# The gap of the matrix rotations: one subtraction on VectorE in place of a matrix product, and a product with A on GpSimd

## Chip, cores and metric

One core of one Trainium2 chip. The metric is the device time in microseconds of one execution of the whole program.

## What is computed

The input is a batch of 16 images with 128 channels of 32x32. Each channel is read as a 32x32 matrix: 2048 matrices. The part that matters here is the first layer of the reference, an eigendecomposition:

```python
def _log_eig(Xf):
    w, V = jnp.linalg.eigh(Xf)
    w = jnp.clip(w, EPS_LOG)
    return jnp.einsum('nij,nj,nkj->nik', V, jnp.log(w), V)
L = _log_eig(Xf)                    # 2048 matrices of 32x32
Lc = gamma * (L - jnp.mean(L, axis=0)) + beta
Y = _exp_eig(Lc)
```

It stands between a group normalisation, and an attention layer (top 32 of 1024 keys) with a mixture of low-rank experts, which the change leaves as they are.

## The kernel before

The stages follow one another, each a block of hand-written engine programs that meet only in semaphores. The stage of the change is `eigen`, from about 245 to 3775 us. It diagonalises all matrices together by **turns**: in each turn, a small rotation is worked out for every matrix from its diagonal and off-diagonal elements, and applied to A (tile `odd`) and to the eigenvectors U (tile `even`). There are 12 turns (`TURNS`) over 32 tiles (`TILES`); a tile has 64 matrices as 128 partitions x 512 columns (four matrices down, 16 across). So there are 384 **slots**, numbered `tau`, and five tiles are in work at once: in slot tau the tile tau has its gaps formed, tile tau-1 its angle (`AT_ANGLE`), tile tau-2 its Gram product (`AT_GRAM`), tile tau-3 its rotation and products (`AT_TURN`), and tile tau-4 is made symmetric again (`AT_SYM`). Turn 11 of the 12 is **mended** (`MEND_AT`, 32 slots): it also restores the orthogonality of U.

Every engine runs its part of the slot in a fixed written order, `slot` on TensorE and `body` on the others, with waits between. The order in a slot without mending:

- TensorE: the product for the rotation's polynomial (`banks[TURN]`, from `zs` and `mix`, L382), the Gram product (x with x, L382), the product of A and the rotation (L382), the gap (L472, L473), the damping (L476, L478), the products that follow (L499). L382 and L499 are 64 products of 32x32 blocks each; the gap and damping products are of full size, 128x128 with 512 columns. The gap bank holds, for each matrix element (i, j), the difference of two diagonal elements: L472 spreads the diagonal over the rows, L473 subtracts it along the columns by a product of minus the identity with `diag_rows`.
- ScalarE: half of the new A (L554), Ln (L557), the new U (L559), Exp (L562), `zs` (L565), the product's copy `prod_u` (L573), the gap's square (L576), the square of the off-diagonal part (L547).
- VectorE: the rotation `j` (L606), `off_rows` (L612), a transpose (L616), `mix` (L619), `rest` (L623), the symmetric A (L627), the angle's tangent `x` = weighed * damped (L634), `weighed` = A * gap (L639), `damped` (L641), `diag_rows` (L593).
- GpSimd: `x_eye` (L663), a copy of U (L668, `u_staged`), a copy of A (L672, `a_staged`), and the masks of the next tile: `diag` (L653) and `off` (L657).

In the mended turn TensorE has two more products, the first of which (`e_flip`) waits for a VectorE transpose (L599) of the copy L668, and the product of A and the rotation comes behind the gap and the damping; L579 copies it out there.

`hold` is a wait that also raises a counter. The loop over the slots is in `through`: the first five slots and the last one of a turn are written out, the others loop.

## Time and profile before

| | |
|---|---|
| median of 3 runs | 9082.76 us (9075.89 to 9084.97) |
| profiled execution | 9074.8 us, its span 9073.1 us |
| TensorE busy | 7923.9 us (87%) |
| VectorE busy | 5380.0 us (59%) |
| ScalarE busy | 3778.8 us (42%) |
| GpSimd busy | 1947.5 us (21%) |
| mean granted TensorE clock | 0.948 |

Busy time is time in which the engine worked on an instruction; the shares are means over stages with different limits. In the rows, PE is TensorE, PEld its load of weights, DVE VectorE, ACT ScalarE, POOL GpSimd. `psum` stands for any bank. A bracket behind a row tells how long the engine had been idle, and what released it.

### The profile page before, as it was taken

How to read it: one execution, taken by the hardware profiler on the slowest of the kernel's cores; microseconds unless marked ns; L12 is line 12 of the kernel's file. 1: busy time of each engine (PE TensorE's matmuls, PEld its weight loads, DVE VectorE, ACT ScalarE, POOL GpSimd, SP SyncE). 2: the span in 40 equal slices, each digit the busy share in tenths (PEclk: the TensorE clock that was granted, in tenths of full speed). 3: DMA queues.
4: the chain of work that ended last, by engine and by line, in shares of the span. 5: the costliest groups of instructions: out<-in, count | busy, mean ns of one | idle time of the engine just before them, and what ended most of it. 6: DMA issues, size and time to landing. Idle time of an engine off the chain costs nothing. (4 is left out here: it accounts for less than half of the span.)

```text
span 9073.1 us, 601301 instructions
## 1 busy us (share of the span) xinstructions
PE 7923.9 (87%) x265196; PEld 4270.7 (47%) x265196; DVE 5380.0 (59%) x15117; ACT 3778.8 (42%) x7262; POOL 1947.5 (21%) x2028
## 2 busy tenths in 40 slices
PE   3999999999999778668856999999999999999998
PEld 2677777777777666557741222222222222222222
DVE  4677777777777546643324555555555555555553
ACT  3455555555555334324422333333334333333333
POOL 1455555555555334300000000000000000000000
PEclk9999999999999889779967999999999999999999
DMA  0000000000000000000010000000000000000000
GB/s 37 1 0 0 0 0 0 0 0 0 0 0 0 0 0 0 1 1 0 0 42 14 15 17 17 12 16 15 13 17 15 17 15 12 17 10 17 15 17 5
DMA packets 58886, 82.10 MB, mean 9 GB/s; under 512 B 26101, under 2 KB 27706, under 8 KB 58426
## 3 DMA queue, kind: packets, MB, share of 16 engines
q1 hardware_dynamic: 58426, 76.45, 3.2%
q8 instruction: 229, 3.75, 0.2%
q14 instruction: 231, 1.89, 0.1%
HBM read 17.63 MB, written 8.39 MB: 3 GB/s over the span
## 5 line engine op out<-in xcount | busy, mean ns | idle before, releaser
L1867 DVE MAX8 w_best<-psum 128x8 f32<-128x128 f32 x8192 | 1725.0, 283 | 1301.9 <-PE psum L1409 1300.5
L1850 ACT ACTIVATE w_exp<-psum 128x512 f32<-128x512 f32 x2048 | 1220.1, 596 | 2291.7 <-PE psum L1418 2289.4
L1428 PE MATMUL psum<-w_exp,w_v 128*32 128x512 f32 x4096 | 2087.6, 608 | 3.0 <-ACT w_inverse L1461 2.7
L1409 PE MATMUL psum<-w_k,w_q 96*128 96x512 bf16 x2048 | 637.3, 394 | 239.7 <-DMA w_k<-w_parts 145.0
L1418 PE MATMUL psum<-w_q,w_k 99*128 99x512 bf16 x2048 | 798.2, 390 | 1.4 <-ACT w_q L1443 1.4
L499 PE MATMUL psum<-e_prod_u,e_j 32*32 32x64 f32 x49152 | 769.8, 215 | 30.5 <-ACT e_prod_u L579 25.1
L499 PEld LDWEIGHTS psum<-e_prod_u,e_j 32*32 32x32 f32 x49152 | 708.0, 105 | 183.2 <-issue 183.2
L1409 PEld LDWEIGHTS psum<-w_k,w_q 96*128 96x128 bf16 x2048 | 123.7, 98 | 1071.4 <-issue 1071.2
L1428 PEld LDWEIGHTS psum<-w_exp,w_v 128*32 128x32 f32 x4096 | 276.0, 108 | 716.8 <-issue 716.8
L653 POOL TENSOR_TENSOR e_diag<-odd,e_eye 128x512 f32<-128x512 f32 x384 | 488.0, 1271 | 559.4 <-PE psum L473 521.3
L547 ACT ACTIVATE e_square<-e_off 128x512 bf16<-128x512 f32 x384 | 242.1, 630 | 844.0 <-POOL e_off L657 844.0
L1418 PEld LDWEIGHTS psum<-w_q,w_k 99*128 99x128 bf16 x2048 | 204.1, 100 | 790.8 <-issue 675.3
L382 PE MATMUL psum<-e_mix,e_zs 32*32 32x32 f32 x49152 | 509.8, 196 | 61.6 <-issue 60.0
L606 DVE TENSOR_TENSOR e_j<-e_rest,psum 128x512 f32<-128x512 f32 x384 | 264.0, 687 | 470.4 <-PE psum L382 470.4
L382 PEld LDWEIGHTS psum<-e_mix,e_zs 32*32 32x32 f32 x49152 | 477.5, 107 | 108.7 <-issue 108.4
L382 PE MATMUL psum<-e_x 32*32 32x32 f32 x49152 | 505.1, 195 | 14.6 <-issue 14.3
L382 PE MATMUL psum<-e_j,e_a_fixed 32*32 32x32 f32 x49152 | 495.9, 194 | 19.6 <-issue 12.7
L951 PE MATMUL psum<-power 32*32 32x32 f32 x28672 | 391.5, 205 | 118.6 <-issue 111.6
L382 PEld LDWEIGHTS psum<-e_j,e_a_fixed 32*32 32x32 f32 x49152 | 462.5, 104 | 62.6 <-issue 28.1
L663 POOL TENSOR_TENSOR e_x_eye<-e_x,e_eye 128x512 f32<-128x512 f32 x384 | 487.8, 1270 | 2.4 <-DVE e_x L634 2.4
L657 POOL TENSOR_TENSOR e_off<-odd,e_not_eye 128x512 f32<-128x512 f32 x384 | 487.9, 1271 | 0.0
L382 PEld LDWEIGHTS psum<-e_x 32*32 32x32 f32 x49152 | 472.5, 106 | 29.6 <-issue 16.3
(268 smaller groups left out, 10889.3 us busy)
## 6 DMA issues: line engine op xcount, KB each, us to landing
w_q<-w_parts SPq DMA_DIRECT2D x768, 32.0 KB, 2.0
w_k<-w_parts SPq DMA_DIRECT2D x768, 32.0 KB, 2.0
odd<-in_x SPq DMA_DIRECT2D x1, 8192.0 KB, 23.1
even<-in_x SPq DMA_DIRECT2D x1, 8192.0 KB, 23.2
out<-w_t SPq DMA_DIRECT2D x16, 512.0 KB, 2.6
w_hid<-in_fc SPq DMA_DIRECT2D x2, 256.0 KB
w_wo<-in_wo SPq DMA_DIRECT2D x8, 8.0 KB
w_wq<-in_wq SPq DMA_DIRECT2D x1, 64.0 KB
```

Of the source, the lines that this page charges most:

```text
L382: last = nc.tensor.matmul(bank[rows, cols], left[rows, cols], right[rows, cols], start=True, stop=True)
L499: last = nc.tensor.matmul(halves(e.pair[:, k // HALF, :])[rows, :, to], e.j[rows, cols], e.prod_u[rows, :, cols], start=True, stop=True)
L606: nc.vector.tensor_tensor(e.j[:], e.rest[:], banks[TURN], ALU.add).then_inc(turned, 1)
L653: nc.gpsimd.tensor_tensor(as_matrices(e.diag[:]), as_matrices(e.a_at(t)), over_matrices(e.eye[:]), ALU.mult)\
L657: nc.gpsimd.tensor_tensor(as_matrices(e.off[:]), as_matrices(e.a_at(t)), over_matrices(e.not_eye[:]), ALU.mult)\
L663: nc.gpsimd.tensor_tensor(as_matrices(e.x_eye[:]), as_matrices(e.x[:]), over_matrices(e.eye[:]), ALU.add)\
L951: last = nc.tensor.matmul(banks[EXP_BANK[n]][rows, S * k:S * k + S], left[rows, k, :], right[rows, k, :], start=True, stop=True)
L1409: last = nc.tensor.matmul(banks[base + k], w.q[0:DEPTH, 4 * g + j, q0:q0 + P], w.k[0:DEPTH, 4 * g + j, half(k)], start=True, stop=True)
L1418: nc.tensor.matmul(banks[4 + x % 2], w.k[0:DEPTH + SHIFT_ROWS, 4 * g + j, P * kt:P * kt + P], w.q[0:DEPTH + SHIFT_ROWS, 4 * g + j, half(qb ...
L1428: nc.tensor.matmul(banks[7][slot(j), :], w.v[:, kt, 4 * g + j, :], w.exp[x % 4][:], start=(kt == 0), stop=(kt == KT - 1)).then_inc(s.weigh ...
L1850: nc.scalar.activation(w.exp[x % 4][:], banks[4 + x % 2], ACT.Exp).then_inc(s.exp_done, 1)
L1867: last = nc.vector.max(w.best[:, i, o, :], banks[o // 4][:, P * (o % 4):P * (o % 4) + P])
```

## The change

The gap no longer ends in an accumulating product. TensorE makes L472's product alone (L477 after); VectorE subtracts `diag_rows` from the bank, spread over the columns, and writes the new tile `gap` (L650). ScalarE squares that tile (L583). GpSimd multiplies A with it (`weighed`, L696), as the last step of its slot, which VectorE did before. On VectorE `x` (L634 in both) moves ahead of `rest` and of the symmetric A, and `diag_rows` (L600 after) ahead of `damped` (L657 after). The tile `minus_ident` and the instruction that fills it are gone, with the counts of the waits around it.

```diff
--- before.py
+++ after.py
@@ -184,7 +184,6 @@
 
     def __init__(self, nc, mem, sb):
         self.block_ones = sb("e_block_ones", [P, P])
-        self.minus_ident = sb("e_minus_ident", [P, P])
         self.damp = [sb(f"e_damp{n}", [P, P], BF16) for n in range(2)]
         self.damp_ident = [sb(f"e_damp_ident{n}", [P, P], BF16) for n in range(2)]
         self.eye = sb("e_eye", [P, S])
@@ -206,6 +205,7 @@
         self.off, self.gap_sq, self.weighed, self.damped = (sb("e_" + n, [P, W]) for n in ("off", "gap_sq", "weighed", "damped"))
         self.half, self.flipped_half, self.flip, self.mend = (sb("e_" + n, [P, W]) for n in ("half", "flipped_half", "flip", "mend"))
         self.prod_u = sb("e_prod_u", [P, 2, W])
+        self.gap = sb("e_gap", [P, W])
         self.square = sb("e_square", [P, W], BF16)
         self.diag_rows = sb("e_diag_rows", [P, TILE])
         self.off_rows = sb("e_off_rows", [P, TILE], BF16)
@@ -265,29 +265,28 @@
             dve.wait_ge(filled, 5)
             folded = "p (q j) -> p j q"
             nc.vector.tensor_reduce(e.eye[:], mem.ident[:].rearrange(folded, j=S), AX.X, ALU.add).then_inc(copied, 1)
-            nc.vector.tensor_scalar(e.minus_ident[:], mem.ident[:], -1.0, None, ALU.mult).then_inc(copied, 1)
             nc.vector.tensor_reduce(e.ramp[:, 0:1], triangle[:], AX.X, ALU.add).then_inc(copied, 1)
-            dve.wait_ge(copied, 3)
+            dve.wait_ge(copied, 2)
...
@@ -453,6 +452,12 @@
         def vectors_at(m):
             return m * 2 + 2
 
+        def mix_at(m):
+            return m * 2 + 1
+
+        def rest_at(m):
+            return m * 2 + 2
+
         def diag_rows_at(m):
             return m * 2 + 1
 
@@ -466,13 +471,13 @@
                 quads(nc, banks[GRAM], e.x, e.x).then_inc(gram_done, 1)
 
             def gaps(m, which, first=False):
-                hold(pe, rows_ready, diag_rows_at(m))
+                hold(pe, diag_ready, m + 1)
+                if not first:
+                    hold(pe, gap_ready, m)
+                nc.tensor.matmul(banks[GAP], e.block_ones[:], e.diag[:], start=True, stop=True).then_inc(gap_done, 1)
+                hold(pe, square_ready, m + 1)
                 if not first:
                     hold(pe, damped, m)
-                nc.tensor.matmul(banks[GAP], e.block_ones[:], e.diag[:], start=True, stop=False)
-                nc.tensor.matmul(banks[GAP], e.minus_ident[:], over_columns(e.diag_rows[:]), start=False, stop=True)\
-                    .then_inc(gap_done, 1)
-                hold(pe, square_ready, m + 1)
                 nc.tensor.matmul(banks[DAMP], e.damp[which][:], e.square[:], start=True, stop=False)
                 hold(pe, rows_ready, off_rows_at(m))
                 nc.tensor.matmul(banks[DAMP], e.damp_ident[which][:], over_columns(e.off_rows[:]), start=False, stop=True)\
@@ -506,7 +511,7 @@
                     if mended:
                         hold(pe, flipped, mended_count(m) + 1)
                         quads(nc, banks[MEND], e.flip, e.flip).then_inc(mend_steps, 1)
-                    hold(pe, mixed, m + 1)
+                    hold(pe, mixed, rest_at(m))
                     quads(nc, banks[TURN], e.zs, e.mix).then_inc(turn_done, 1)
                 if has(AT_GRAM):
                     gram(tau - AT_GRAM)
@@ -572,8 +577,10 @@
                         act.wait_ge(prod_done, m + 1)
                         nc.scalar.activation(e.prod_u[:, 0], banks[PROD], ACT.Copy).then_inc(prod_out, 1)
                 if has(0):
-                    act.wait_ge(gap_done, tau + 1)
-                    nc.scalar.activation(e.gap_sq[:], banks[GAP], ACT.Square).then_inc(gap_squared, 1)
+                    act.wait_ge(gap_ready, tau + 1)
+                    if has(AT_ANGLE):
+                        act.wait_ge(damped, tau - AT_ANGLE + 1)
+                    nc.scalar.activation(e.gap_sq[:], e.gap[:], ACT.Square).then_inc(gap_squared, 1)
                 if has(AT_TURN) and mended:
                     act.wait_ge(prod_done, m + 1)
                     nc.scalar.activation(e.prod_u[:, 0], banks[PROD], ACT.Copy).then_inc(prod_out, 1)
@@ -589,7 +596,7 @@
             def rows(m, first=False):
                 dve.wait_ge(diag_ready, m + 1)
                 if not first:
-                    dve.wait_ge(gap_done, m)
+                    dve.wait_ge(gap_ready, m)
                 nc.vector.tensor_reduce(e.diag_rows[:], as_matrices(e.diag[:]), AX.X, ALU.add).then_inc(rows_ready, 1)
 
             def body(tau, j, has, mended):
@@ -616,8 +623,16 @@
                     nc.vector.transpose(e.flipped_half[:], e.half[:]).then_inc(half_flipped, 1)
                 if has(AT_GRAM):
                     dve.wait_ge(gram_out, tau - AT_GRAM + 1)
-                    nc.vector.scalar_tensor_tensor(e.mix[:], banks[GRAM], FOURTH / THIRD, e.x[:], ALU.mult, ALU.add)
+                    nc.vector.scalar_tensor_tensor(e.mix[:], banks[GRAM], FOURTH / THIRD, e.x[:], ALU.mult, ALU.add)\
+                        .then_inc(mixed, 1)
                     dve.wait_ge(eye_added, tau - AT_GRAM + 1)
+                if has(AT_ANGLE):
+                    dve.wait_ge(inverse, tau - AT_ANGLE + 1)
+                    if has(AT_GRAM):
+                        dve.wait_ge(mixed, mix_at(tau - AT_GRAM))
+                    dve.wait_ge(weighed, tau - AT_ANGLE + 1)
+                    nc.vector.tensor_tensor(e.x[:], e.weighed[:], e.damped[:], ALU.mult).then_inc(angle, 1)
+                if has(AT_GRAM):
                     if has(AT_TURN):
                         dve.wait_ge(turned, tau - AT_TURN + 1)
                     nc.vector.scalar_tensor_tensor(e.rest[:], banks[GRAM], -0.5, e.x_eye[:], ALU.mult, ALU.add)\
@@ -626,21 +641,20 @@
                     dve.wait_ge(half_flipped, tau - AT_SYM + 1)
                     nc.vector.tensor_tensor(e.a_at(tile_of(j, AT_SYM)), e.half[:], e.flipped_half[:], ALU.add)\
                         .then_inc(balanced, 1)
-                if has(AT_ANGLE):
-                    dve.wait_ge(inverse, tau - AT_ANGLE + 1)
-                    if has(AT_GRAM):
-                        dve.wait_ge(mixed, tau - AT_GRAM + 1)
-                    dve.wait_ge(weighed, tau - AT_ANGLE + 1)
-                    nc.vector.tensor_tensor(e.x[:], e.weighed[:], e.damped[:], ALU.mult).then_inc(angle, 1)
+                if has(0):
+                    dve.wait_ge(gap_done, tau + 1)
+                    dve.wait_ge(rows_ready, diag_rows_at(tau))
+                    if has(AT_ANGLE):
+                        dve.wait_ge(gap_squared, tau - AT_ANGLE + 1)
+                        dve.wait_ge(weighed, tau - AT_ANGLE + 1)
+                    nc.vector.tensor_tensor(as_matrices(e.gap[:]), as_matrices(banks[GAP]), over_columns(e.diag_rows[:]),
+                                            ALU.subtract).then_inc(gap_ready, 1)
+                if has(AHEAD):
+                    rows(tau + 1)
                 if has(0):
                     dve.wait_ge(gap_squared, tau + 1)
-                    if has(AT_ANGLE):
-                        dve.wait_ge(angle, tau - AT_ANGLE + 1)
-                    nc.vector.tensor_tensor(e.weighed[:], e.a_at(tile_of(j, 0)), banks[GAP], ALU.mult).then_inc(weighed, 1)
                     dve.wait_ge(damp_done, tau + 1)
                     nc.vector.tensor_tensor(e.damped[:], e.gap_sq[:], banks[DAMP], ALU.add).then_inc(damped, 1)
-                if has(AHEAD):
-                    rows(tau + 1)
 
             rows(0, first=True)
             through(dve, body)
@@ -650,6 +664,7 @@
             def masks(m, t, first=False):
                 if not first:
                     hold(pool, gap_done, m)
+                    hold(pool, rows_ready, diag_rows_at(m - 1))
                 nc.gpsimd.tensor_tensor(as_matrices(e.diag[:]), as_matrices(e.a_at(t)), over_matrices(e.eye[:]), ALU.mult)\
                     .then_inc(diag_ready, 1)
                 if not first:
@@ -660,6 +675,8 @@
             def body(tau, j, has, mended):
                 if has(AT_GRAM):
                     hold(pool, angle, tau - AT_GRAM + 1)
+                    if has(AT_TURN):
+                        hold(pool, mixed, rest_at(tau - AT_TURN))
                     nc.gpsimd.tensor_tensor(as_matrices(e.x_eye[:]), as_matrices(e.x[:]), over_matrices(e.eye[:]), ALU.add)\
                         .then_inc(eye_added, 1)
                 if has(AT_TURN):
@@ -672,6 +689,11 @@
                     nc.gpsimd.tensor_copy(e.a_fixed[:], e.a_at(tile_of(j, AT_GRAM))).then_inc(a_staged, 1)
                 if has(AHEAD):
                     masks(tau + 1, tile_of(j, AHEAD))
+                if has(0):
+                    hold(pool, gap_ready, tau + 1)
+                    if has(AT_ANGLE):
+                        hold(pool, angle, tau - AT_ANGLE + 1)
+                    nc.gpsimd.tensor_tensor(e.weighed[:], e.a_at(tile_of(j, 0)), e.gap[:], ALU.mult).then_inc(weighed, 1)
 
             masks(0, 0, first=True)
             through(pool, body)
```

VectorE, one unmended slot as it is written out, before (the names are written<-read):

```order
L606 TENSOR_TENSOR e_j<-e_rest,psum 128x512
L612 TENSOR_REDUCE e_off_rows<-e_square 128x16
L616 STREAM_TRANSPOSE e_flipped_half<-e_half 128x512
L619 SCALAR_TENSOR_TENSOR e_mix<-psum,e_x 128x512
L623 SCALAR_TENSOR_TENSOR e_rest<-psum,e_x_eye 128x512
L627 TENSOR_TENSOR odd<-e_half,e_flipped_half 128x512
L634 TENSOR_TENSOR e_x<-e_weighed,e_damped 128x512
L639 TENSOR_TENSOR e_weighed<-odd,psum 128x512
L641 TENSOR_TENSOR e_damped<-e_gap_sq,psum 128x512
L593 TENSOR_REDUCE e_diag_rows<-e_diag 128x16
```

and the same slot of the changed kernel:

```order
L613 TENSOR_TENSOR e_j<-e_rest,psum 128x512
L619 TENSOR_REDUCE e_off_rows<-e_square 128x16
L623 STREAM_TRANSPOSE e_flipped_half<-e_half 128x512
L626 SCALAR_TENSOR_TENSOR e_mix<-psum,e_x 128x512
L634 TENSOR_TENSOR e_x<-e_weighed,e_damped 128x512
L638 SCALAR_TENSOR_TENSOR e_rest<-psum,e_x_eye 128x512
L642 TENSOR_TENSOR odd<-e_half,e_flipped_half 128x512
L650 TENSOR_TENSOR e_gap<-psum,e_diag_rows 128x512
L600 TENSOR_REDUCE e_diag_rows<-e_diag 128x16
L657 TENSOR_TENSOR e_damped<-e_gap_sq,psum 128x512
```

There are ten instructions in both; `x` has moved up by two places, the new `gap` stands where `weighed` stood, and `damped` has become the last.

GpSimd, the same slot of the changed kernel (before, the first five of these rows stand there, under L663, L668, L672, L653 and L657):

```order
L680 TENSOR_TENSOR e_x_eye<-e_x,e_eye 128x512
L685 COPY e_prod_u<-even 128x512
L689 COPY e_a_fixed<-odd 128x512
L668 TENSOR_TENSOR e_diag<-odd,e_eye 128x512
L672 TENSOR_TENSOR e_off<-odd,e_not_eye 128x512
L696 TENSOR_TENSOR e_weighed<-odd,e_gap 128x512
```

The sixth row is new, between `off` of this slot and `x_eye` of the next.

## Rows read from the trace of the kernel before

**Rows 1.** Windows: busy time of each engine in two stretches; columns in the first line.
```profile
core 0: us, PE busy (x) PEld busy (x) DVE busy (x) ACT busy (x) POOL busy (x), PEclk, DMA share, GB/s
1330.00:2400.00 1070.00, 1030.07 (x65764) 798.98 (x65753) 796.75 (x1270) 559.87 (x1016) 620.80 (x636) 1.00 0.00 0
2955.00:3470.00 515.00, 379.30 (x24733) 317.22 (x24723) 251.58 (x390) 167.19 (x295) 159.84 (x165) 0.86 0.00 0
```

**Rows 2.** One line's instructions: count, duration ns min/median/max, first and last start.
```profile
L576 ACT ACTIVATE e_gap_sq<-psum x177: 597/597/598, 1425.8 to 2899.0; 128x512 f32<-128x512 f32 x177
...
L579 ACT ACTIVATE e_prod_u<-psum x32: 597/597/598, 2989.4 to 3480.2; 128x512 f32<-128x512 f32 x32
```

**Rows 3.** Timeline, one unmended slot, TensorE: start us, us, engine, line.
```profile
1503.57 1.28 PE L382 MATMUL psum<-e_mix,e_zs 32*32 32x32 f32 x128 [0.16 <-issue]
...
1506.09 1.28 PE L382 MATMUL psum<-e_j,e_a_fixed 32*32 32x32 f32 x128
...
1507.47 1.10 PE L472 MATMUL psum<-e_diag,e_block_ones 128*128 128x512 f32 x2
...
1508.40 1.02 PE L473 MATMUL psum<-e_diag_rows,e_minus_ident 128*128 128x512 f32 x2
...
1509.26 0.38 PE L476 MATMUL psum<-e_square,e_damp 128*128 128x512 bf16 x1
...
1509.79 1.99 PE L499 MATMUL psum<-e_prod_u,e_j 32*32 32x64 f32 x128
...
1511.93 1.28 PE L382 MATMUL psum<-e_mix,e_zs 32*32 32x32 f32 x128 [0.16 <-issue]
```

**Rows 4.** The same timeline, GpSimd.
```profile
1507.63 0.61 POOL L672 COPY e_a_fixed<-odd 128x512 f32 x1 [2.02 <-PE psum L382]
...
1509.69 1.27 POOL L653 TENSOR_TENSOR e_diag<-odd,e_eye 128x512 f32<-128x512 f32 x1 [1.46 <-PE psum L473]
...
1510.92 1.28 POOL L657 TENSOR_TENSOR e_off<-odd,e_not_eye 128x512 f32<-128x512 f32 x1
...
1512.15 1.27 POOL L663 TENSOR_TENSOR e_x_eye<-e_x,e_eye 128x512 f32<-128x512 f32 x1
```

**Rows 5.** The same timeline, VectorE and ScalarE.
```profile
1504.88 0.71 ACT L557 ACTIVATE e_damped<-e_damped,e_floor 128x512 f32<-128x512 f32 x1
1504.89 0.69 DVE L606 TENSOR_TENSOR e_j<-e_rest,psum 128x512 f32<-128x512 f32 x1 [1.18 <-PE psum L382]
...
1507.11 0.69 DVE L619 SCALAR_TENSOR_TENSOR e_mix<-psum,e_x 128x512 f32<-128x512 f32 x1 [0.32 <-ACT e_zs L565]
...
1508.92 0.68 DVE L634 TENSOR_TENSOR e_x<-e_weighed,e_damped 128x512 f32<-128x512 f32 x1
...
1509.46 0.60 ACT L576 ACTIVATE e_gap_sq<-psum 128x512 f32<-128x512 f32 x1 [1.46 <-PE psum L473]
...
1510.20 0.69 DVE L639 TENSOR_TENSOR e_weighed<-odd,psum 128x512 f32<-128x512 f32 x1 [0.60 <-ACT e_gap_sq L576]
```

**Rows 6.** Timeline, three places where GpSimd and VectorE ran at once.
```profile
264.07 1.26 POOL L657 TENSOR_TENSOR e_off<-odd,e_not_eye 128x512 f32<-128x512 f32 x1
264.37 1.52 DVE L634 TENSOR_TENSOR e_x<-e_weighed,e_damped 128x512 f32<-128x512 f32 x1
...
3775.09 0.61 POOL L731 COPY e_a_fixed<-even 128x512 f32<-128x512 f32 x1 [12.32 <-SPq L682]
3775.12 1.12 DVE L701 TENSOR_TENSOR e_zs<-odd,e_eye 128x512 f32<-128x512 f32 x1 [0.33 <-PEq L413]
3775.64 1.07 POOL L731 COPY e_rest<-even 128x512 f32<-128x512 f32 x1
...
3824.55 0.69 DVE L715 TENSOR_TENSOR e_x<-even,e_level 128x512 f32 x1 [3.77 <-PE psum L382]
3824.61 1.11 POOL L731 COPY e_a_fixed<-even 128x512 f32 x1 [47.89 <-PE psum L382]
```

**Rows 7.** Timeline, one slot of the mended turn.
```profile
3223.66 1.29 PE L382 MATMUL psum<-e_j,e_a_fixed 32*32 32x32 f32 x128
...
3229.44 0.61 POOL L668 COPY e_prod_u<-even 128x512 f32 x1
...
3230.94 1.93 PE L382 MATMUL psum<-e_flip 32*32 32x32 f32 x128 [3.22 <-DVE e_flip L599]
```

More of the change, by code:

```diff
@@ L276, in _ @@
             for n, value in enumerate((FIRST_DAMP, LATER_DAMP)):
+                dve.wait_ge(copied, 5 + 3 * n)
+                nc.vector.tensor_scalar(spare[:], mem.ident[:], KAPPA / value, None, ALU.mult).then_inc(copied, 1)
                 dve.wait_ge(copied, 6 + 3 * n)
-                nc.vector.tensor_scalar(spare[:], mem.ident[:], KAPPA / value, None, ALU.mult).then_inc(copied, 1)
+                nc.vector.tensor_tensor(spare[:], spare[:], e.block_ones[:], ALU.add).then_inc(copied, 1)
                 dve.wait_ge(copied, 7 + 3 * n)
-                nc.vector.tensor_tensor(spare[:], spare[:], e.block_ones[:], ALU.add).then_inc(copied, 1)
-                dve.wait_ge(copied, 8 + 3 * n)
                 nc.vector.tensor_scalar(e.damp[n][:], spare[:], value, None, ALU.mult).then_inc(copied, 1)
@@ L284, in _ @@
                 nc.vector.tensor_scalar(e.damp_ident[n][:], mem.ident[:], value, None, ALU.mult).then_inc(copied, 1)
-            dve.wait_ge(copied, 14)
+            dve.wait_ge(copied, 13)
             dve.wait_ge(summed, 1)
@@ L289, in _ @@
                 .then_inc(copied, 1)
-            dve.wait_ge(copied, 15)
+            dve.wait_ge(copied, 14)
             nc.vector.tensor_reduce(e.mirror_rows[:], e.mirror[:].rearrange(folded, j=S), AX.X, ALU.add).then_inc(copied, 1)
@@ L418, in eigen @@
                                                                             "e_rows_ready"))
-        gap_done, damp_done, gap_squared, damped = (sem(n) for n in ("e_gap_done", "e_damp_done", "e_gap_squared",
-                                                                     "e_damped"))
+        gap_done, damp_done, gap_ready, gap_squared, damped = (sem(n) for n in ("e_gap_done", "e_damp_done", "e_gap_ready",
+                                                                                "e_gap_squared", "e_damped"))
         weighed, log_taken, inverse, angle, eye_added = (sem(n) for n in ("e_weighed", "e_log_taken", "e_inverse", "e_angle",
```

## The prediction

> **What bounds the kernel now.** The windows come first, as the page's shares mix stages. In the stretch of unmended turns TensorE is busy for 1030 of 1070 us at a granted clock of 1.00, its upper level, while VectorE has 797 and GpSimd 621 [rows 1]. So look for work that can leave TensorE. In the mended turn TensorE has only 379 of 515 us, at a clock of 0.86: something else sets the pace. The starts of one line give the length of a slot: unmended (2899.0-1425.8)/176 = 8.37 us; mended (3480.2-2989.4)/31 = 15.83 us [rows 2]. Then the timeline of one slot; I count its times from the start of the TURN product, 1503.57. TensorE goes from product to product and has 0.16 us idle in the whole slot, before the next TURN at 8.36 [rows 3]. TensorE bounds 352 of the 384 slots.
>
> **The change, part by part.** *The product L473.* It starts at 4.83 and the damping at 5.69 [rows 3]: its removal frees 0.86 us. The most it can give is the other pair's 0.93 (3.90 to 4.83) [rows 3]. The damping then starts at 4.83, the last product L499 at 5.36 (was 6.22), and the slot is 7.50 long, if nobody else is later. The wait that is added ahead of the damping lies under the gap's product.
>
> *Who else must now fit into 7.50.* GpSimd: the pitch of its big multiplications is 1.23 (1509.69 to 1510.92), a copy takes 0.61 [rows 4]. Before, 3x1.23 + 2x0.61 = 4.9; with `weighed` one more: 6.14. That fits, and `weighed` is a product of the same size; I give it 1.23. A time up to 2.5 would still fit. Queued behind it on GpSimd are `x_eye` and the copies; they have room, as the copy of A waits for the product of A anyway (2.02 us idle before it) [rows 4]. VectorE has ten instructions before and after, at a pitch of 0.61; only `weighed` (0.69, one operand in the bank) turns into the subtraction, same shape, also from the bank, at the same price [rows 5].
>
> *The chain through VectorE and ScalarE.* The gap's end moves from 5.85 (4.83+1.02) to 3.90+1.10 = 5.00 [rows 3]; GpSimd's `diag` started 0.27 behind it [rows 3, 4], so now at 5.27, and ends at 6.54. Chain in the new order: `mix` at 3.54 [rows 5], then `x`, `rest`, A, gap at 0.61 each, the gap's end, square 0.60 and `damped` 0.68 with some 0.1 for the two hand-overs; then from the Ln's start to the next `mix` 2.23 (1504.88 to 1507.11) [rows 5]. Sum 4x0.61 + 0.69 + 0.60 + 0.68 + 0.1 + 2.23 = 6.7, under 7.50. TensorE stays the bound by this count, but it leaves out one thing.
>
> *GpSimd and VectorE at once.* [Rows 6] show that some of their instructions do not overlap. `x`, which has both inputs in SBUF, took 1.52 us instead of 0.68 where it started inside a GpSimd multiplication: that one ended at 265.33, and `x` 0.56 later. The other way round, a GpSimd copy that started 0.06 behind such a VectorE instruction took 1.11 instead of 0.61, until 0.48 after VectorE's end. Before, `x` and the symmetric A run from 1508.32 to 1509.60, in GpSimd's pause (1508.24 to 1509.69) [rows 4, 5]: they never met. Now `x` comes at 4.15, inside the copy of A (4.06 to 4.67), and ends at 5.22. `rest` ends at 5.8; the symmetric A then meets `diag` (5.27 to 6.54) and ends at 7.10. The gap ends at 7.70; `diag_rows` and the square at 8.3; `damped` at 9.1, which is 1.6 of the next slot. There Ln starts at about 1.8 instead of 1.31 (the square of the off part, held back too, and the half of A are ahead of it), `mix` at 4.1, and `x` at 4.7, now free of the copy: the delay does not grow. `j` can start at 1.5 instead of 1.32 and ends at 2.2; the product of A, at 2.52, finds it ready. GpSimd's `off` is held until 7.10, plus 1.14 (1.27 less the 0.13 that the copy in rows 6 saved): 8.24; `weighed`, `x_eye` and the copy of U then end at about 11.2, and the copy of A starts at 7.50+4.06 = 11.56. All fits, with 0.3 us left in the tightest place. The Trainium skill has this as a rule (SBUF — State Buffer, Who interferes with whom): a VectorE instruction with two SBUF inputs contends with a GpSimd instruction that reads SBUF, and the second one blocks fully until the first ends. The trace agrees (1.52 beside 0.68). The rule does not say who goes next when a second GpSimd instruction is queued behind the first.
>
> That is the open point, and one place shows it: a VectorE instruction came at 3775.12 inside a GpSimd copy that ended at 3775.70, the next copy's record starts at 3775.64, and VectorE ended at 3776.24, the second copy at 3776.71 [rows 6]. So VectorE got in between two back-to-back GpSimd instructions. I take that for the forecast. Gain: 352 x 0.86 = 303 us.
>
> *The mended turn.* Its loop runs from the product of A on TensorE through GpSimd (copy of A, `diag`, `off`, `x_eye`, copy of U) and the transpose on VectorE to the first product: 3223.66 to 3230.94, with TensorE idle for 3.22 us at its end [rows 7]. From there TensorE runs through its products to the product of A again. `weighed` now stands in the GpSimd part: +1.23. The pair L473 leaves the TensorE part: -0.86. Per slot +0.37, 32 slots: +12 us. TensorE's pause grows by about a microsecond, and the product after it already runs at the lower level of 1.2 GHz (1.93 us beside 1.28 at the upper) [rows 3, 7]. The bounds of the extra: nothing, or one more product of this kind at the lower level in each slot, 0.65x32 = 21 us. I take the middle, +10, since the pause is only a third longer.
>
> *The rest* (constants, the stages behind) loses one small instruction: nothing. Filling the first slots has a longer latency of a few microseconds, inside the uncertainty.
>
> **Sum.** -303 + 12 + 10 = -281 us. The profiled execution took 9074.8, so 8794; the median is 8 us above it, so 9082.8 - 281 = **8802 us**.
>
> **The rivals.**
>
> *A, slower: GpSimd goes on with what is queued, and the waiting VectorE is let in only when GpSimd stops.* The symmetric A waits until the end of `off`. Counted from the start of `diag`: `off` ends at 2.49, A at 3.04, the gap at 3.64, the square at 4.3, `damped` at 5.0; `j`, queued behind it, runs to 5.69, TensorE takes it 0.15 later, and from the product of A to the next `diag` it is 1.38+1.10+0.27 = 2.75. The loop is 8.59 us, over the 8.37 of now: +0.22x352 = +77, plus 22 for the mended turn, 9182 us. It decides once the symmetric A starts only behind `off`; break-even is at a slot of 8.31. Against it stands the one place at 3775 us; for it, that it is one place, of copies and not multiplications.
>
> *B, a mixed form.* The symmetric A misses its turn in some slots, or another wait eats the 0.3 us. Every second slot in form A gives (7.50+8.59)/2 = 8.05: gain 0.32x352 = 113, less 22: 8992 us. One in three gives 7.86: 8925. For it: little room is left. Against it: a delayed slot gives ScalarE and VectorE a whole microsecond to catch up.
>
> *C, no change.* The product is hidden anyway: that would need TensorE to wait in the slot, and it has 0.16 us of idle time [rows 3]. 9083 us.
>
> *D.* A reader may also fear GpSimd as the new bound. At 6.14 + one blocked instruction's 0.5 it is under 7.50; it would need two more blockings in a slot.
>
> **How the numbers follow.** A measurement of this kernel tells 0.2%, some 18 us, from no change. Forecast (with up to one slot in three late) 0.78; B beyond that 0.08; C 0.03; A, with other mishaps that cost time, 0.11. So faster 0.86, same 0.03, slower 0.11. The low end: 0.93 x 352 = 327 us without any price in the mended turn, 8756, up to 8760. The high end is the mixed form with one in three, 8925, up to 8930. D's chance is inside B.
>
> **What would show it.** Right: a slot of 7.5 us (the starts of the gap's square on ScalarE), TensorE busy in over 95% of the unmended stretch, the damping 0.93 behind the gap's product, the symmetric A with a mean of about 1.3 us instead of 0.68, `weighed` on GpSimd at 1.27, and a mended slot of 16.2 to 16.8. Wrong: idle time before the product of A that `j` ends, or before L657 that the gap's square ends; the symmetric A at over 2 us; a slot of 8.6 us; a GpSimd multiplication with two full inputs of well over 1.27 us. If GpSimd and VectorE do overlap freely, the slot is the same, and only the reasons fail.

## The result and the profile after

The changed kernel takes 8841.12 us (median of 4 runs, 8838.98 to 8844.09), the one before, measured beside it, 9083.59 us. The ratio is 0.9733, with a 95% interval of 0.9721 to 0.9746: 242 us faster. The forecast of 8802 us was 39 us too low; the range (8760 to 8930) holds the result.

The starts of the gap's square on ScalarE, and of the copy of the product of A in the mended turn, in the trace after (they answer to [rows 2]):

```profile
L583 ACT ACTIVATE e_gap_sq<-e_gap x155: 630/631/634, 1421.8 to 2599.3; 128x512 f32<-128x512 f32 x155
...
L586 ACT ACTIVATE e_prod_u<-psum x32: 578/579/597, 2750.2 to 3267.0; 128x512 f32<-128x512 f32 x32
```

An unmended slot is (2599.3-1421.8)/154 = 7.65 us instead of 8.37; a mended one (3267.0-2750.2)/31 = 16.67 instead of 15.83. 352 x 0.72 = 253 us won, 32 x 0.84 = 27 lost: 226, beside 231 by which the spans of the two profiled executions differ (9073.1 and 8842.4). From its first to its last gap's square the stage takes 3479.5 us before (251.3 to 3730.8) and 3247.5 after (249.9 to 3497.4), 232 less; so the 6 us beyond 226 lie inside the stage, outside its regular slots, and the other stages stayed as they were, to within 3 us.

The windows of an unmended stretch and of the mended turn (busy us of each engine, count, then the granted TensorE clock), which answer to [rows 1]:

```profile
1330.00:2200.00 870.00, 816.85 (x58625) 671.55 (x58728) 782.63 (x1139) 482.86 (x912) 750.22 (x684) 1.00 0.00 0
2750.00:3270.00 520.00, 350.32 (x24073) 309.24 (x24096) 241.79 (x374) 156.98 (x281) 191.59 (x190) 0.82 0.00 0
```

GpSimd is busy in 750 of 870 us (86%, was 58%), VectorE in 783 (90%, was 74%), TensorE in 817 (94%, was 96%). Now three engines are nearly full, and each instruction that one of them holds up on another counts.

The timeline of one slot after; its TensorE rows answer to [rows 3], the others to [rows 4, 5]:

```profile
1505.13 0.68 DVE L650 TENSOR_TENSOR e_gap<-psum,e_diag_rows 128x512 f32<-128x512 f32 x1
...
1505.53 1.28 PE L381 MATMUL psum<-e_mix,e_zs 32*32 32x32 f32 x128 [0.18 <-issue]
...
1505.84 0.63 ACT L583 ACTIVATE e_gap_sq<-e_gap 128x512 f32<-128x512 f32 x1 [3.42 <-DVE e_gap L650]
...
1505.91 0.69 DVE L600 TENSOR_REDUCE e_diag_rows<-e_diag 128x16 f32<-128x512 f32 x1
...
1506.51 0.68 DVE L657 TENSOR_TENSOR e_damped<-e_gap_sq,psum 128x512 f32<-128x512 f32 x1
1506.76 1.28 PE L381 MATMUL psum<-e_x 32*32 32x32 f32 x128
...
1507.11 0.68 DVE L613 TENSOR_TENSOR e_j<-e_rest,psum 128x512 f32<-128x512 f32 x1
...
1508.14 1.28 PE L381 MATMUL psum<-e_j,e_a_fixed 32*32 32x32 f32 x128
...
1509.55 1.10 PE L477 MATMUL psum<-e_diag,e_block_ones 128*128 128x512 f32 x2
...
1509.62 0.69 DVE L626 SCALAR_TENSOR_TENSOR e_mix<-psum,e_x 128x512 f32<-128x512 f32 x1 [0.62 <-ACT e_zs L570]
...
1510.52 0.69 DVE L634 TENSOR_TENSOR e_x<-e_weighed,e_damped 128x512 f32<-128x512 f32 x1 [0.20 <-DVE e_mix L626]
...
1510.99 1.34 POOL L668 TENSOR_TENSOR e_diag<-odd,e_eye 128x512 f32<-128x512 f32 x1 [0.79 <-PE psum L477]
...
1511.01 1.99 PE L504 MATMUL psum<-e_prod_u,e_j 32*32 32x64 f32 x128
...
1511.72 1.16 DVE L642 TENSOR_TENSOR odd<-e_half,e_flipped_half 128x512 f32<-128x512 f32 x1
1512.29 1.72 POOL L672 TENSOR_TENSOR e_off<-odd,e_not_eye 128x512 f32<-128x512 f32 x1
1512.81 0.68 DVE L650 TENSOR_TENSOR e_gap<-psum,e_diag_rows 128x512 f32<-128x512 f32 x1
...
1513.17 1.28 PE L381 MATMUL psum<-e_mix,e_zs 32*32 32x32 f32 x128 [0.18 <-issue]
```

From the product of A (1508.14) to L477 it is 1.41 us, from there to L504 1.46, to the next TURN 2.16, and from TURN to the product of A 2.61: 7.64. Before, the same pieces are 1.38, 2.32, 2.14 and 2.52 [rows 3]. So L473's 0.86 is gone in full, and 0.14 has come back, 0.09 of it ahead of the product of A.

### The profile page after: what moved, and what is told of

Read it like the earlier page. It is cut to its first block and busy times, and to the rows that moved or that the text cites. A ratio compares the mean times of both kernels' runs of the same rounds, so it can differ in the third digit from the quotient of the medians.

```text
span 8842.4 us, 603547 instructions
## 1 busy us (share of the span) xinstructions
PE 7580.9 (86%) x264045; PEld 4140.3 (47%) x264428; DVE 5585.1 (63%) x15116; ACT 3724.2 (42%) x7262; POOL 2585.4 (29%) x2412
## 5 line engine op out<-in xcount | busy, mean ns | idle before, releaser
L504 PE MATMUL psum<-e_prod_u,e_j 32*32 32x64 f32 x49152 | 771.3, 216 | 35.7 <-ACT e_prod_u L586 31.6
L504 PEld LDWEIGHTS psum<-e_prod_u,e_j 32*32 32x32 f32 x49152 | 709.2, 105 | 188.9 <-issue 188.9
L583 ACT ACTIVATE e_gap_sq<-e_gap 128x512 f32<-128x512 f32 x384 | 242.3, 631 | 1250.1 <-DVE e_gap L650 1250.1
L672 POOL TENSOR_TENSOR e_off<-odd,e_not_eye 128x512 f32<-128x512 f32 x384 | 643.1, 1675 | 0.0
L668 POOL TENSOR_TENSOR e_diag<-odd,e_eye 128x512 f32<-128x512 f32 x384 | 491.5, 1280 | 310.8 <-PE psum L477 272.5
L680 POOL TENSOR_TENSOR e_x_eye<-e_x,e_eye 128x512 f32<-128x512 f32 x384 | 490.5, 1277 | 0.0
L696 POOL TENSOR_TENSOR e_weighed<-odd,e_gap 128x512 f32<-128x512 f32 x384 | 489.5, 1275 | 3.5 <-DVE e_gap L650 3.5
```

The costliest lines, as they stand in the source:

```text
L504: last = nc.tensor.matmul(halves(e.pair[:, k // HALF, :])[rows, :, to], e.j[rows, cols], e.prod_u[rows, :, cols], start=True, stop=True)
L668: nc.gpsimd.tensor_tensor(as_matrices(e.diag[:]), as_matrices(e.a_at(t)), over_matrices(e.eye[:]), ALU.mult)\
L672: nc.gpsimd.tensor_tensor(as_matrices(e.off[:]), as_matrices(e.a_at(t)), over_matrices(e.not_eye[:]), ALU.mult)\
L680: nc.gpsimd.tensor_tensor(as_matrices(e.x_eye[:]), as_matrices(e.x[:]), over_matrices(e.eye[:]), ALU.add)\
L696: nc.gpsimd.tensor_tensor(e.weighed[:], e.a_at(tile_of(j, 0)), e.gap[:], ALU.mult).then_inc(weighed, 1)
```

## The experiments

A ring is a closed loop of waits that comes back to its own start one slot later; the slot can't be shorter than one round of it. Theory 1: the 0.15 us over the forecast slot are a ring through VectorE (`diag`, symmetric A, gap, `diag_rows`, `damped`, `j`, product of A, gap product, `diag`). Theory 2: they are on TensorE's own queue, the order in which it works off its instructions and waits. Times are medians of the runs, slots from the starts of the gap's square between 1420 and 2600 us, mended slots from the copy of the product of A.

| label | edit | time us | unmended slot | mended slot |
|---|---|---|---|---|
| before | | 9083.6 | 8.37 | 15.83 |
| the change | | 8841.1 | 7.65 | 16.67 |
| x_back | x behind the symmetric A | 8955.9 | 7.98 | 16.61 |
| gap_first | gap ahead of the symmetric A | 8851.3 | 7.69 | 16.63 |
| one_input | symmetric A with one SBUF input | (8859.1) | 7.65 | 16.60 |
| weigh_dve | weighed on VectorE | 9305.1 | 9.08 | 15.46 |
| before_two | before, with the common counter | 9111.0 | 8.48 | 15.46 |
| own_mix | own counter for mix | 8844.8 | 7.68 | 16.35 |
| pool_order | weighed behind the copy of U | 8799.8 | 7.65 | 15.28 |
| own_mix_pool | the last two | 8788.8 | 7.68 | 14.52 |
| own_one | own_mix and one_input | (8806.8) | 7.55 | 16.51 |
| own_a_early | own_mix, symmetric A between mix and x | 8805.2 | 7.55 | 16.46 |
| all_three | own_a_early and pool_order | 8755.4 | 7.55 | 14.94 |

In brackets: the adding of the transpose is left out there, and only one run was timed. The times come from four series on the chip; the kernel before, measured in each, had medians of 9083.6 (the change), 9082.0 (x_back to weigh_dve), 9077.1 (before_two to own_mix_pool) and 9085.6 us (the rest).

**The third part undone: x_back.**

In this diff and those below, a name in capitals stands for the whole block of VectorE's program that forms the tile: `x`, `rest`, the symmetric A (BALANCE), the gap, `diag_rows` (ROWS), `damped`.

```diff
- X; REST; BALANCE; GAP; ROWS; DAMPED
+ REST; BALANCE; X; GAP; ROWS; DAMPED
```

> The angle's x back behind the symmetric A on VectorE; all else as changed. Theory 1: the slot of 7.65 us is a ring through VectorE (diag on GpSimd, symmetric A, gap, diag_rows, damped, j, product of A on TensorE, gap product, diag). Then A starts at 5.3 ahead of diag, but x meets diag and waits until its end near 7.1: the gap ends 0.3 us later, slot 7.9 to 8.0, about 8940 us. Theory 2: TensorE's own queue with its added waits makes the 7.65, the order on VectorE is hidden: slot 7.65, 8841 us.

Measured: slot (2592.7-1420.2)/147 = 7.98 us, 8955.9 us; ratio to before 0.9861 (0.9845 to 0.9878). Theory 1 had the slot (7.9 to 8.0) and the time to within 16 us. The timeline of all three engines:

```profile
1502.19 1.28 PE L381 MATMUL psum<-e_j,e_a_fixed 32*32 32x32 f32 x128 [0.43 <-DVE e_j L613]
...
1504.89 0.68 DVE L636 TENSOR_TENSOR odd<-e_half,e_flipped_half 128x512 f32 x1
...
1505.14 1.56 POOL L668 TENSOR_TENSOR e_diag<-odd,e_eye 128x512 f32<-128x512 f32 x1 [0.79 <-PE psum L477]
...
1505.49 1.76 DVE L643 TENSOR_TENSOR e_x<-e_weighed,e_damped 128x512 f32<-128x512 f32 x1
```

`x` came 0.35 us behind the start of `diag` and took 1.76 us. `diag` itself had come inside the symmetric A and took 1.56. TensorE waits 0.43 us for `j` ahead of the product of A. So moving `x` up is worth 0.33 us in each slot, 115 us of the change's 242: without it the change wins half. That there is a ring through VectorE at 7.98 in this order does not yet say what holds the changed kernel's 7.65.

**The gap ahead of the symmetric A: gap_first.**

```diff
- X; REST; BALANCE; GAP; ROWS; DAMPED
+ X; REST; GAP; BALANCE; ROWS; DAMPED
```

> VectorE's subtraction (gap) ahead of the symmetric A, so that the instruction that GpSimd's diag holds up is no longer ahead of the gap; same instructions. Theory 1 (ring through VectorE): the ring is cut, TensorE's 7.50 us is left: slot 7.50 to 7.55, 352 x 0.12 to 0.15 less, 8788 to 8800 us. Theory 2 (TensorE's own queue): slot 7.65, 8841 us.

Measured: 8851.3 us (8847.4 to 8862.4), slot (2599.7-1423.8)/153 = 7.69. The expectation of theory 1 fell: the ring is shorter, but nothing is won. Of the 150 slots between 1430 and 2590 us, 126 are 7.62 long and 24 are 7.96 to 8.13. Why TensorE gains only 0.02 us in the many is shown further below; what happens in the few is seen in two slots in a row:

```profile
1500.26 0.68 DVE L650 TENSOR_TENSOR odd<-e_half,e_flipped_half 128x512 f32<-128x512 f32 x1
1500.34 1.74 POOL L672 TENSOR_TENSOR e_off<-odd,e_not_eye 128x512 f32<-128x512 f32 x1
...
1508.03 1.27 POOL L672 TENSOR_TENSOR e_off<-odd,e_not_eye 128x512 f32<-128x512 f32 x1
1508.06 1.80 DVE L650 TENSOR_TENSOR odd<-e_half,e_flipped_half 128x512 f32<-128x512 f32 x1
```

In one slot the symmetric A comes 0.08 us ahead of `off` and takes 0.68. In the next it comes 0.03 us behind it and takes 1.80. The 24 slots with the long form (1.79 or 1.80) are the 24 long slots. That is the form of rival B, in one slot of six: who is first decides 1.1 us for VectorE, and about 0.4 us for the slot.

**Is it the shared access? one_input.**

```diff
-  tensor_tensor(a, half, flipped_half, add)
+  scalar_tensor_tensor(a, banks[GAP], 0.0, half, mult, add)   # half copied with scale 1
```

> The symmetric A is formed with one SBUF input: half plus 0 times the gap bank, and half is copied with scale 1; the adding of the transpose is left out, so the time behind the eigen stage is not to be compared, only the slot. Theory 1 with the shared access as its cause: the instruction takes 0.69 us instead of 1.16 to 1.29, GpSimd's off 1.27 instead of 1.72, and the slot is 7.50 to 7.55. If the long instruction has another cause (an address register, the 32 KB row it writes), it stays at 1.2 and the slot at 7.65.

One line each, this kernel's symmetric A and `off` first (duration ns min/median/max), then those of the changed kernel:

```profile
L644 DVE SCALAR_TENSOR_TENSOR odd<-psum,e_half x384: 672/675/692, 290.0 to 3538.8; 128x512 f32 x156, 128x512 f32<-128x512 f32 x36
...
L675 POOL TENSOR_TENSOR e_off<-odd,e_not_eye x384: 1263/1277/1719, 248.2 to 3489.4; 128x512 f32<-128x512 f32 x192
```

```profile
L642 DVE TENSOR_TENSOR odd<-e_half,e_flipped_half x384: 679/1292/1510, 285.0 to 3538.1; 128x512 f32 x156, 128x512 f32<-128x512 f32 x36
...
L672 POOL TENSOR_TENSOR e_off<-odd,e_not_eye x384: 1262/1721/1736, 246.6 to 3489.0; 128x512 f32<-128x512 f32 x192
```

With one SBUF input, the instruction takes 675 ns instead of 1292, and `off` 1277 instead of 1721. So it is the second SBUF input, as [rows 6] had suggested and as the Trainium skill has it (SBUF — State Buffer, Who interferes with whom). But the slot stays at (2592.8-1422.8)/153 = 7.65, and `j` now waits for TensorE:

```profile
1501.14 0.69 DVE L613 TENSOR_TENSOR e_j<-e_rest,psum 128x512 f32<-128x512 f32 x1 [0.57 <-PE psum L381]
...
1502.43 1.28 PE L381 MATMUL psum<-e_j,e_a_fixed 32*32 32x32 f32 x128
```

`j` has ended at 1501.83 and the product of A starts 0.6 us later, 1.38 behind the Gram product at 1501.05. VectorE is not what it waits for here. That speaks for theory 2.

**The subtraction part alone: weigh_dve.**

```diff
 ROWS
+ weighed = A * gap      (VectorE; gone from GpSimd)
 DAMPED
```

> The subtraction part alone: the product of A and the gap stays on VectorE (now with two SBUF inputs), GpSimd has five instructions again, x stays ahead. Theory 1: eleven instructions on VectorE's ring and one more that GpSimd holds up: slot 8.3 to 8.6, less 1.23 in a mended slot (15.5); 9050 to 9130 us, nothing of the gain is left. Theory 2: TensorE bounds as before, slot 7.65 and the mended slots cheaper: 8800 us.

Measured: 9305.1 us, slot (2599.9-1419.5)/130 = 9.08; ratio to before 1.0250 (1.0232 to 1.0267), slower than before and worse than expected. The mended slot did what was expected: (3682.1-3202.8)/31 = 15.46. The timeline of the unmended slot:

```profile
1501.41 1.27 POOL L685 TENSOR_TENSOR e_x_eye<-e_x,e_eye 128x512 f32<-128x512 f32 x1
1501.63 1.60 DVE L658 TENSOR_TENSOR e_weighed<-odd,e_gap 128x512 f32<-128x512 f32 x1
...
1503.76 0.67 DVE L613 TENSOR_TENSOR e_j<-e_rest,psum 128x512 f32<-128x512 f32 x1
...
1504.72 1.68 PE L381 MATMUL psum<-e_j,e_a_fixed 32*32 32x32 f32 x128 [1.61 <-DVE e_j L613]
...
1506.34 2.08 PE L477 MATMUL psum<-e_diag,e_block_ones 128*128 128x512 f32 x2
```

`weighed` with two SBUF inputs meets `x_eye` and takes 1.60 instead of 0.69, `j` is late, and TensorE waits 1.61 us for it. The kind was expected, the size was not: `damped` follows `weighed` 1.53 us later (1501.63 to 1503.16), so the ring of 7.65 gets about 1.5 longer, where the expectation had 0.65 to 0.95.

In the last row the gap's product takes 2.08 us instead of 1.10: the trace has the granted clock at its lower level from 1505.2 to 1508.6, and 0.94 is its mean in the unmended stretch, where it is 1.00 in the changed kernel. That isn't what makes the slot long. The long gap product (1.57 to 2.08) stands in 41 of 130 slots, and these are 9.05 us long in the mean, the others 9.08: what TensorE loses at the lower level comes out of its next wait for `j`, which is 0.1 to 0.4 us behind each of these 41 slots and 1.5 to 1.7 behind 85 of the other 88.

**TensorE's queue: before_two.** The waits of TensorE in the order of its instructions have one row more in the changed kernel: a register instruction (ALU_OP) ahead of the product of A and the rotation, at 1507.78 in the slot shown above. Before, `mixed` counted one per slot, and its value served the wait on `turned` too; in the change, `mix` and `rest` raise the same counter.

```diff
   mix = ...                              
+      .then_inc(mixed, 1)
-  hold(pe, mixed, m + 1)
+  hold(pe, mixed, m * 2 + 2)
```

(the wait of `x` counts in the same way)

> The kernel before, with one thing of the change: mix raises the counter that rest raises, so that waits on it count two per slot, and TensorE computes one more wait value in a register, ahead of the product of A and the rotation. No work is added or moved. Theory 2 (TensorE's sequencer pays for it): slot 8.46 us instead of 8.37, the product of A 1.38 behind the Gram product instead of 1.29, 0.09 x 352 = +32 us, 9114 us. Theory 1 (a ring through VectorE makes the 7.65): no difference to before, 9082 us.

Measured: 9111.0 us beside 9077.1, ratio 1.0041 (1.0027 to 1.0054): slower, by 34 us. The slot is (2598.4-1420.2)/139 = 8.48. The total is near the expected 32 partly by chance: the unmended slots lose 37 us, the mended turn gives 12 back (15.46 instead of 15.83, at a granted clock of 0.93 instead of 0.87), and some 9 of the 35 us between the two spans lie behind the eigen stage, where the kernels are the same. The slot is the evidence. In its timeline

```profile
1500.18 1.28 PE L382 MATMUL psum<-e_x 32*32 32x32 f32 x128
1501.56 1.28 PE L382 MATMUL psum<-e_j,e_a_fixed 32*32 32x32 f32 x128
1502.93 1.10 PE L472 MATMUL psum<-e_diag,e_block_ones 128*128 128x512 f32 x2
```

the product of A is 1.38 behind the Gram product. From TURN to it was 2.52 in [rows 3], of which 1.23 belong to the Gram product, so 1.29 (the Gram product started 1.23 behind TURN in the slot shown above, too). One register instruction on TensorE, between two runs of 64 small products, costs 0.09 us there, and 0.01 to 0.02 more elsewhere in the slot.

**The repair: own_mix.**

```diff
-  mix = ...  .then_inc(mixed, 1)
+  mix = ...  .then_inc(mix_made, 1)
-  hold(pe, mixed, rest_at(m))     # m * 2 + 2
+  hold(pe, mixed, rest_at(m))     # m + 1
```

> The changed kernel, with a counter of its own for mix, so that TensorE's waits count one per slot again and its extra register instruction is gone. Theory 2: slot 7.56 instead of 7.65, 0.09 x 352 = -32 us, 8810 us. Theory 1: 7.65 and 8841 us. If both are close to each other, something between: a ring at 7.6.

Measured: 8844.8 us, slot (2592.7-1426.1)/152 = 7.68: no gain. In its timeline

```profile
1503.71 1.28 PE L381 MATMUL psum<-e_x 32*32 32x32 f32 x128
...
1504.14 0.68 DVE L614 TENSOR_TENSOR e_j<-e_rest,psum 128x512 f32<-128x512 f32 x1
...
1505.12 1.28 PE L381 MATMUL psum<-e_j,e_a_fixed 32*32 32x32 f32 x128
...
1506.50 1.10 PE L478 MATMUL psum<-e_diag,e_block_ones 128*128 128x512 f32 x2
...
1507.55 0.69 DVE L635 TENSOR_TENSOR e_x<-e_weighed,e_damped 128x512 f32<-128x512 f32 x1 [0.20 <-DVE e_mix L627]
...
1507.95 1.42 POOL L669 TENSOR_TENSOR e_diag<-odd,e_eye 128x512 f32<-128x512 f32 x1 [0.76 <-PE psum L478]
```

`j` has no idle time before it, ends at 1504.82, and the product of A follows 0.30 later: 1.41 behind the Gram product. Now the ring holds it. So neither theory is right alone. Theory 3: both bounds lie at 7.65 to 7.68, and taking away one shows the other. The ring is even 0.03 longer here than the changed kernel's slot: `x` idles 0.20 us behind `mix` in all 114 slots between 1330 and 2200 us, in the changed kernel in 9 of 114, and where it is still running when `diag` comes, `diag` takes longer (1.32 us in the median here, 1.27 there). That is the likely reason. Why the new counter makes `x` later is not shown.

**The mended turn: pool_order and own_mix_pool.**

```diff
  x_eye; copy of U
+ weighed of the slot before
  copy of A; diag; off
- weighed
```

> The changed kernel, with the product of A and the gap on GpSimd moved behind the copy of U of the next slot: out of the mended turn's loop, same number of instructions. Mended slot 16.65 down by 1.23 to 15.4, 32 slots: -39 us; the unmended slot 7.65 as before, as x comes later than the product: 8802 us. Rival: the gap's tile is free later or x waits, the unmended slot grows by over 0.11 and it all is lost.

> Both of the last two edits. Additive if neither touches the other's loop: 8841 - 32 - 39 = 8770 us, slot 7.56 and 15.4. If the product of A and the gap next to x becomes the bound once TensorE is faster: slot 7.65, 8802 us.

Measured: pool_order 8799.8 us, the mended slot (3224.4-2750.6)/31 = 15.28, the unmended (2592.4-1422.3)/153 = 7.65. The expectation holds in all three numbers. own_mix_pool takes 8788.8 us (slot 7.68); 8770 was expected. own_mix's 32 us did not come, and part of that is made up by the mended slot: (3209.4-2759.3)/31 = 14.52, 0.76 under pool_order's with the same GpSimd order.

The granted clock goes with most of this difference. Over the mended turn it is 0.92 in own_mix_pool and 0.84 in pool_order. Sorted by the clock granted in each, rounded to a tenth, mended slots last, in us (number of slots in brackets):

| mended slot at a clock of | 0.8 | 0.9 | 1.0 |
|---|---|---|---|
| before | 16.37 (9) | 15.70 (20) | 14.70 (2) |
| the change | 16.81 (24) | 16.17 (7) | |
| pool_order | 15.68 (13) | 15.00 (18) | |
| own_mix_pool | | 14.81 (18) | 13.88 (12) |

(One slot of own_mix_pool, 16.91 at 0.7, is left out.) At equal clock own_mix_pool is within 0.2 us of pool_order; it has 12 slots at full clock, pool_order none. What decides how many there are is not shown. At equal clock `weighed` costs the mended loop 1.1 to 1.2 us, where 1.23 was expected.

**Both bounds away: own_one and own_a_early.** own_one is own_mix with one_input's edit. own_a_early has the full result:

```diff
  mix
+ BALANCE
  X; REST
- BALANCE
  GAP; ROWS; DAMPED
```

> The changed kernel with both suspected bounds away: mix has its own counter (no extra register instruction on TensorE), and the symmetric A has one SBUF input (the adding of the transpose is left out, so only the slot is to be read). Theory 3 (two bounds almost equal, TensorE's queue at 7.65 and the ring through VectorE at 7.65): only both edits together shorten the slot, to 7.50 to 7.57. If a third thing holds 7.65, it stays.

> The own counter for mix, and the symmetric A moved to between mix and x on VectorE, where GpSimd's copy of A ends; the result is the full one. Theory 3: A takes about 0.7 instead of 1.16 us, the gap ends 0.7 us earlier, the ring is cut as in the run with one input, and TensorE is left as the bound: slot 7.50 to 7.57, 352 x 0.10 = -35 us against the changed kernel, 8805 us. Rival: x then meets diag and holds GpSimd, the slot stays at 7.65.

Measured: own_one has a slot of (2593.5-1423.5)/155 = 7.55, own_a_early of (2592.5-1422.5)/155 = 7.55, at 8805.2 us (8805 was expected; ratio to before 0.9691, 0.9676 to 0.9706). The timeline of own_a_early:

```profile
1501.03 1.28 PE L381 MATMUL psum<-e_j,e_a_fixed 32*32 32x32 f32 x128
...
1502.41 1.10 PE L478 MATMUL psum<-e_diag,e_block_ones 128*128 128x512 f32 x2
...
1503.02 0.68 DVE L632 TENSOR_TENSOR odd<-e_half,e_flipped_half 128x512 f32<-128x512 f32 x1
...
1503.61 0.69 DVE L639 TENSOR_TENSOR e_x<-e_weighed,e_damped 128x512 f32<-128x512 f32 x1
1503.85 1.58 POOL L669 TENSOR_TENSOR e_diag<-odd,e_eye 128x512 f32<-128x512 f32 x1 [0.76 <-PE psum L478]
...
1504.82 0.68 DVE L651 TENSOR_TENSOR e_gap<-psum,e_diag_rows 128x512 f32<-128x512 f32 x1
...
1507.29 1.28 PE L381 MATMUL psum<-e_x 32*32 32x32 f32 x128
1507.38 0.69 DVE L614 TENSOR_TENSOR e_j<-e_rest,psum 128x512 f32<-128x512 f32 x1 [0.50 <-PE psum L381]
```

The symmetric A now takes 0.68 us: it starts as GpSimd's copy of A is about to end. `diag` meets `x` and takes 1.58, with nobody waiting. The gap starts 2.41 behind L478 (3.26 behind L477 in the changed kernel), and `j` waits 0.50 for TensorE. Theory 3 holds: with the own counter alone (own_mix) or the ring shortened alone (one_input) nothing was won, with both 0.10 us per slot. The early symmetric A was not run without the own counter; one_input stands in for it.

**A version that beats both: all_three.**

> The own counter, the early symmetric A, and the product of A and the gap behind the copy of U on GpSimd. Additive: slot 7.50 to 7.57 and a mended slot of 14.4 to 15.3: 8788 - 35 = 8750 us. If GpSimd's order now meets x (its product ends later than x wants it), the slot stays at 7.65 and the time at 8788.

Measured: 8755.4 us (8751.9 to 8756.5), ratio 0.9636 (0.9622 to 0.9649): 330 us under the kernel before, 86 under the change; slot (2599.0-1421.1)/156 = 7.55, mended slot (3180.7-2717.7)/31 = 14.94. All three lie where they were expected.

## Why the prediction was right, and where it was off

- *The bound and the gain.* Right: TensorE bounded the unmended slot, and L473's 0.86 us left it in full. This is the bulk of the gain.
- *The order of VectorE and GpSimd at once.* Right in kind: the symmetric A waits for `diag` (1.16 us in the slot shown, "about 1.3" was forecast, the median is 1.292), and VectorE is let in between two GpSimd instructions: A came at 1511.72 inside `diag` (1510.99 to 1512.33), `off` was queued, A ended at 1512.88 and `off` at 1514.01. So rival A did not happen. weigh_dve shows what a longer meeting would have cost.
- *The term that was mis-sized: 0.86 per slot, in full.* "The slot is 7.50 long, if nobody else is later." It is 7.65: some 50 us of gain are missing. 0.10 of the 0.15 has two causes, each of which alone keeps the slot at 7.65 or above. The first I did not look at: the order of TensorE's instructions showed one register instruction more, and I costed waits, not the computing of their values. It measured 0.09 to 0.11 (before_two, and own_one beside one_input, 7.55 and 7.65). The second is the ring, "0.3 us left in the tightest place". From the prediction's own times one round of it is 9.7+0.15-2.52 = 7.33, so 0.17 was left, not 0.3; in own_mix, where it sets the pace, it is 7.68. Two terms of it were too small. TensorE starts 0.30 behind the end of `j`, not 0.15. And `diag` ends 1.76 (median) behind the end of the gap's product, not 1.54: it starts 0.34 behind the product's end instead of 0.27 in the slots shown, where the change has given GpSimd a third wait ahead of it (the likely reason, but no run takes it out), and it takes longer where it meets the end of `x` (1.34 in the slot shown), as `x` must wait for `mix`. `diag_rows` is late too (0.78 behind the gap instead of 0.61), but that costs the ring nearly nothing: `damped` behind it also needs the gap's square, which ended 0.04 ahead of its start (1506.47 and 1506.51). The last 0.05 of the 0.15 stays in own_a_early (7.55): 0.01 is rounding, and 0.04 lies between L504 and the next TURN (a median of 2.19 us from start to start, 2.15 before). No run shows what it is.
- *The mended turn.* Right in kind, and near in size by some luck. +22 us was forecast with the clock, 27 measured. At equal granted clock the mended slot grew by 0.44 to 0.47 (forecast +0.37), the rest of the 0.84 is the lower clock, 0.82 instead of 0.87 over the turn. But before_two moved this turn by 12 us through the clock alone, so a miss or a hit of that size says little. That `weighed` is in this loop is shown by pool_order, which takes it out and wins 1.39 us per mended slot, 1.1 to 1.2 of it at equal clock.
- *The signs.* The symmetric A, `weighed` (1.275 us, median) and the mended slot came as announced; the slot of 7.5 and a TensorE that is busy in over 95% of the unmended stretch (94%) did not. Of the signs of being wrong, idle time that `j` ends and a symmetric A over 2 us did not show in the unmended stretch. `off` took 1.72 us, which is its wait for the symmetric A, as in the prediction's own count (about 6.5 to 8.24).
- *The rivals.* B's form did not appear in the changed kernel's unmended slots (all of 7.64 to 7.68 between 1430 and 2590 us), but in gap_first. C and A did not occur. D: GpSimd was busy for 86%; it was not the bound.
- *The sum.* -281 forecast, -242 measured: 50 us too much in the unmended slots and 5 in the mended ones; 226 are left, beside 231 by the spans (the difference lies at the ends of the turns and outside the stage); 12 of the 242 by the medians are the place of the profiled executions in their runs (9074.8 beside 9083.6 before, 8844.1 beside 8841.1 after).

## What to carry to other kernels

When an engine's work shrinks, the next bounds can lie close together (7.65 and 7.68 us here). An experiment that removes one and shows no gain has not refuted it; remove both. Ahead of moving work to GpSimd, list which VectorE instructions have two SBUF inputs, and put them where GpSimd pauses or is about to end: one place was worth 0.33 us per slot here. A place a few hundredths of a microsecond ahead of a GpSimd instruction is no safe place (gap_first). And on a queue of many small instructions, count the register instructions: two events on one counter made a wait's value cost 0.1 us. Where a stage's clock differs between two kernels, compare slots at equal clock before giving a difference a cause.

## What was not expected of the hardware

- A VectorE instruction that must wait for GpSimd is let in at the end of the running GpSimd instruction, though the next one is queued: no symmetric A of the changed kernel took over 1.51 us, where a wait for `off` too would make it 2.4 or more (an estimate: the 0.6 of `diag` left when it comes, 1.24 of `off`, and 0.55). The next one then took 1.72 instead of 1.27.
- A few hundredths of a microsecond in arrival decide 1.1 us (0.68 when up to 0.08 ahead, 1.80 when 0.03 behind, gap_first).
- One register instruction between runs of small products costs TensorE 0.09 us, at a clock of 1.00 (before_two).
- With waits of 1.5 to 1.7 us in an otherwise full slot, TensorE's granted clock fell to the lower level in 41 of 130 slots (weigh_dve; the gap's product 2.08 us beside 1.10), and the time did not show it: these slots were as long as the others.
- The mended turn ran at a mean clock of 0.87 in one kernel and 0.93 in another in which no work was moved (before, before_two), and was 12 us shorter.
